# Key masks multiplied out on GpSimd, and the key scan split in two, in an attention and routing kernel

## What is computed

```python
feature_keep = min(HEAD_DIM, max(1, math.ceil(HEAD_DIM * (k_keep / Tx))))   # 16 * 64 / 1024 -> 1
q = _sparsify_last_dim_topk(proj(wq), feature_keep)   # one feature of 16 is kept
k = _sparsify_last_dim_topk(proj(wk), feature_keep)
v = _sparsify_last_dim_topk(proj(wv), feature_keep)
scores = einsum('bhqd,bhkd->bhqk', q, k) / sqrt(HEAD_DIM)       # causal
topk_vals, topk_idx = top_k(scores, 64)                         # 64 keys for each query
attn = softmax(scatter(topk_vals, topk_idx))
out = einsum('bhqk,bhkd->bhqd', attn, v)
```

## Time and profile before

| | before |
|---|---|
| median of 3 runs | 1072.18 us (1070.66 to 1073.46) |
| the profiled execution | 1072.58 us, of which the span from first to last instruction is 1070.7 us |
| attention part, 16 groups | some 66 to 730 us of the span |
| experts | from some 740 us to the end |
| granted TensorE clock, mean | 0.912 |

### The profile page before, as it was taken

How to read it: one execution, slowest core, us unless ns; L and a number is a source line. 1 busy time by engine, 2 the same in 40 slices (tenths; PEclk the granted TensorE clock), 3 DMA queues, 4 the chain that set the end, 5 groups by cost and what they waited for, 6 DMA issues and landing times. The chain is left out here.

```text
span 1070.7 us, 17237 instructions
## 1 busy us (share of the span) xinstructions
PE 919.0 (86%) x6504; PEld 497.5 (46%) x6504; DVE 662.1 (62%) x1462; ACT 480.0 (45%) x631; POOL 270.0 (25%) x403
## 2 busy tenths in 40 slices
PE   6778999898999888999999999996213999999996
PEld 4533443334444453534335445335102666666664
DVE  6758667567677666686784784625486655543441
ACT  2635667764667746476665554661000122221110
POOL 3503212411322402132320210001003433334222
PEclk9779999999999989999988998897555999999999
DMA  4000000000100001100002012001651144442211
GB/s 149 10 1 21 1 21 1 2 1 2 60 21 1 1 27 56 60 1 2 2 1 81 2 41 81 1 1 40 219 197 41 46 114 105 113 114 40 25 20 20
DMA packets 34854, 46.57 MB, mean 43 GB/s; under 512 B 2184, under 2 KB 30928, under 8 KB 34640
## 3 DMA queue, kind: packets, MB, share of 16 engines
q1 hardware_dynamic: 28624, 36.89, 10.3%
q0 software_dynamic: 6144, 8.52, 4.9%
HBM read 32.69 MB, written 12.72 MB: 42 GB/s over the span
## 5 line engine op out<-in xcount | busy, mean ns | idle before, releaser
L947 ACT ACTIVATE p_buf<-ps 128x1024 f32<-128x1024 f32 x288 | 279.4, 1023 | 182.7 <-PE ps L424 98.7
L424 PE MATMUL ps<-qx,kd 32*128 32x512 f32 (+3 forms) x1280 | 149.0, 542 | 29.9 <-DVE p_buf L1281 26.1
L457 PE MATMUL ps<-p_buf,vv 128*17 128x512 f32 (+3 forms) x1664 | 160.2, 487 | 0.0
L2096 ACT ACTIVATE h_t<-ps,b_t 128x512 f32<-128x512 f32 x64 | 44.0, 687 | 239.7 <-PE ps L2036 239.7
L1281 DVE SCALAR_TENSOR_TENSOR p_buf<-ps,p_buf 128x1024 f32<-128x1024 f32 x64 | 76.7, 1220 | 76.6 <-ACT p_buf L947 63.5
L2036 PE MATMUL ps<-tok_t,w_sb 128*128 128x512 f32 x256 | 114.2, 605 | 0.5 <-DVEq L2143 0.5
L2046 PE MATMUL ps<-w_sb,h_t 128*128 128x256 f32 x512 | 112.5, 380 | 0.8 <-ACT h_t L2096 0.8
L779 POOL TENSOR_SCALAR_AFFINE_SELECT p_buf<-p_buf 128x512 f32<-128x512 f32 x64 | 42.0, 669 | 274.2 <-ACT p_buf L947 271.5
L2046 PEld LDWEIGHTS ps<-w_sb,h_t 128*128 128x128 f32 x512 | 96.6, 190 | 15.3 <-ACT h_t L2096 1.6
L424 PEld LDWEIGHTS ps<-qx,kd 32*128 32x128 f32 x1280 | 55.8, 193 | 72.5 <-issue 57.1
L365 PE MATMUL ps<-w_t,h_t 128*128 128x512 f32 (+1 forms) x224 | 78.8, 496 | 0.8 <-ACT w_t L889 0.8
(11 more groups left out here) (293 smaller groups left out, 1392.9 us busy)
## 6 DMA issues: line engine op xcount, KB each, us to landing
w_sb<-in_L_ffn_w_dram SPq DMA_DIRECT2D x16, 1024.0 KB, 8.5
h_table<-xr SPq DMA_DIRECT2D x3, 1056.0 KB, 4.6
x_in<-in_L_attn_x_dram SPq DMA_DIRECT2D x6, 512.0 KB, 3.9
out_dram<-xr SPq DMA_DIRECT2D x3, 1024.0 KB, 5.2
xr<-in_L_attn_x_dram SPq DMA_DIRECT2D x3, 1024.0 KB, 5.7
h_table<-xr SPq DMA_DIRECT2D x2, 528.0 KB, 3.1
xr<-in_L_attn_x_dram SPq DMA_DIRECT2D x2, 512.0 KB, 5.4
p_buf<-in_L_wmod_dram SPq DMA_DIRECT2D x1, 1024.0 KB, 8.6
```

The lines of the kernel that those rows point to most:

```text
L424: m = pe.matmul(o, key, qx[r, par, t0:t0 + w], start=True, stop=not early)
L457: m = pe.matmul(ps[32 * h:32 * h + HD + 1, 6, o:o + w], vv[:, (gi // NG) % 2, i, HG * (gi % NG) + h, :], p_of(gi, u)[:, h, lo:lo + w], sta ...
L947: act.activation(p_of(gi, u)[:, 2 * a:2 * a + 2, :], buf(w), ACT.Exp, scale=0.25).then_inc(free_of(w)[0], 1)
L2096: act.activation(h1_t[:, f, :], ps[:, L1_BANKS[f % 3], :], ACT.Relu, bias=b1_t[:, e * FO + f:e * FO + f + 1]).then_inc(s_h1, 1)
```

## The change

The work stays what it was; its order on VectorE changes, and one piece goes to GpSimd.

- `key_counts` becomes `counts_first` (tokens 0 to 511, once K0 is there), in front of the masks `mask(gi, 1, 0)` and `mask(gi, 1, 1)`, and `counts_second` (512 to 1023, carried on), behind the masks and behind `one_feature(b + 1, t0 + 1)`, which went behind the masks too.
- `keys` becomes `key_maxima` and `keys_shifted`. `key_maxima` begins with two small [128, 128] masks, `k_yes` and `k_neg`, and signals `f_yes`. GpSimd's new `key_kinds(n)` waits for that and multiplies them out over the heads into `k_one` and `k_opp`. It stands behind `tri(gi, 2)` and `tri(gi, 3)`, in front of `stage` and of `keep(b + 1, t0 + 1)`. `keys_shifted` waits for it (`f_kinds`) before it shifts `ks` and `kx`.
- `out_rows_of(gi, 0)` stands between the two halves of `keys`; `normalize(b + 1, 0)` follows it. `zero_rank` comes before `queries`, and `losers` before `one_feature(b + 1, t0 + 3)` and `feature_limits`.

```diff
@@ -185,6 +185,8 @@
         l_max = sf("l_max", [P, NT])
 
         onesz = sf("onesz", [P, HG, P], BF16)
+        k_yes = sf("k_yes", [P, P], BF16)
+        k_neg = sf("k_neg", [P, P], BF16)
         sgn = sf("sgn", [P, 1])
         identb = sf("identb", [P, P], BF16)
         take = sf("take", [P, P], BF16)
@@ -223,6 +225,7 @@
         NU = len(UNITS)
         GA = B * NG
         FIRST = (1, 4)
+        f_yes, f_kinds = sem("f_yes"), sem("f_kinds")
 
 
         ring_at, m_at, pv_at = {}, {}, {}
@@ -780,6 +783,14 @@
                         lo += w
                     m.then_inc(f_tri, 1)
 
+                def key_kinds(n):
+                    pool.wait_ge(f_yes, n)
+
+                    pool.wait_ge(f_mfull, m_at["W", n - 1] + 1)
+                    pool.tensor_tensor(k_one[:, :, :], k_yes[:, :].unsqueeze(1).to_broadcast([P, HG, P]), onesz[:, :, :], ALU.mult)
+                    pool.tensor_tensor(k_opp[:, :, :], k_neg[:, :].unsqueeze(1).to_broadcast([P, HG, P]), onesz[:, :, :], ALU.mult)
+                    pool.drain().then_inc(f_kinds, 1)
+
                 def keep(b, t):
                     pool.wait_ge(f_one, NT * b + t + 1)
                     pool.wait_ge(*free_of(("Y", b, t)))
@@ -861,6 +872,8 @@
                         keep(b + 1, t0)
                     tri(gi, 2)
                     tri(gi, 3)
+                    if gi + 1 < GA:
+                        key_kinds(gi + 1)
                     if g == 0 or g == 3 and pre:
                         stage(gi + 2)
                     if tiles:
@@ -1216,31 +1229,45 @@
                     dve.tensor_tensor(y_most[:, :], y_most[:, :], y_ext[:, 2:3], ALU.max)
                     dve.drain()
 
-                def key_counts(n):
-                    kx = kd[:, n % 2, :]
+                def counts_first(n):
+                    h = slice(0, 512)
+                    dve.wait_ge(f_mfree, m_at["K0", n] + 1)
+                    dve.tensor_scalar(k_not[:, h], kd[:, n % 2, h], 0.0, None, ALU.is_le)
+                    dve.drain()
+                    dve.tensor_tensor_scan(left[:, h], k_not[:, h], minus1[:, :].to_broadcast([P, 512]), TOPK + 0.5,
+                                           ALU.add, ALU.add)
+
+                def counts_second(n):
+                    h = slice(512, T)
                     dve.wait_ge(f_mfree, m_at["K1", n] + 1)
-                    dve.tensor_scalar(k_not[:, :], kx, 0.0, None, ALU.is_le)
-                    dve.drain()
-                    dve.tensor_tensor_scan(left[:, :], k_not[:, :], minus1[:, :].to_broadcast([P, T]), TOPK + 0.5,
+                    dve.drain()
+                    dve.tensor_copy(carry[:, :], left[:, 511:512])
+                    dve.tensor_scalar(k_not[:, h], kd[:, n % 2, h], 0.0, None, ALU.is_le)
+                    dve.drain()
+                    dve.tensor_tensor_scan(left[:, h], k_not[:, h], minus1[:, :].to_broadcast([P, 512]), carry[:, :],
                                            ALU.add, ALU.add)
                     dve.drain().then_inc(f_cnr, 1)
 
-                def keys(n):
-                    par = n % 2
-                    kx = kd[:, par, :]
+                def key_maxima(n):
+                    kx = kd[:, n % 2, :]
+                    dve.tensor_scalar(k_yes[:, :], kx[:, 0:P], 0.0, None, ALU.is_gt)
+                    dve.tensor_scalar(k_neg[:, :], ks[:, n % 2, :], 0.0, None, ALU.is_lt).then_inc(f_yes, 1)
+
 
                     dve.tensor_tensor_scan(mx[:, :], kx[:, 0:512], kx[:, 0:512], 0.0, ALU.max, ALU.max)
                     dve.tensor_reduce(k_max1[:, :], kx[:, 512:T], AX.X, ALU.max)
                     dve.tensor_scalar(k_far[:, :], k_not[:, :], -FAR, None, ALU.mult)
                     dve.tensor_tensor(n_lo[:, :], n_lo[:, :], left[:, T - 1:T], ALU.min)
                     dve.scalar_tensor_tensor(kb[:, :], k_not[:, 0:P], FAR, kx[:, 0:P], ALU.mult, ALU.add)
-                    dve.scalar_tensor_tensor(k_one[:, :, :], kx[:, 0:P].unsqueeze(1).to_broadcast([P, HG, P]), 0.0,
-                                             onesz[:, :, :], ALU.is_gt, ALU.mult)
-                    dve.scalar_tensor_tensor(k_opp[:, :, :], ks[:, par, :].unsqueeze(1).to_broadcast([P, HG, P]), 0.0,
-                                             onesz[:, :, :], ALU.is_lt, ALU.mult)
                     dve.drain()
                     dve.tensor_tensor(k_max[:, :], mx[:, 511:512], k_max1[:, :], ALU.max)
-                    dve.drain()
+
+                def keys_shifted(n):
+                    par = n % 2
+                    kx = kd[:, par, :]
+                    dve.drain()
+
+                    dve.wait_ge(f_kinds, n)
                     dve.tensor_scalar(ks[:, par, :], ks[:, par, :], k_max[:, :], None, ALU.subtract)
                     dve.scalar_tensor_tensor(kx, kx, k_max[:, :], k_far[:, :], ALU.subtract, ALU.add).then_inc(f_kp, 1)
 
@@ -1447,42 +1474,46 @@
                     if gi:
                         out_rows_of(gi - 1, 1)
                     if more:
-                        key_counts(n)
-                    if g == 0 and pre:
-                        normalize(b + 1, 0)
+                        counts_first(n)
+                    mask(gi, 1, 0)
+                    mask(gi, 1, 1)
                     if tiles:
                         one_feature(b + 1, t0 + 1)
-                    mask(gi, 1, 0)
-                    mask(gi, 1, 1)
+                    if more:
+                        counts_second(n)
                     if post and g == norm_group(b - 1):
                         second_norm(b - 1, 1)
                     if g == 1 and pre:
                         norm_stats(b + 1, 1)
                     if more:
-                        keys(n)
-                    if tiles:
-                        one_feature(b + 1, t0 + 2)
+                        key_maxima(n)
                     out_rows_of(gi, 0)
+                    if g == 0 and pre:
+                        normalize(b + 1, 0)
                     if g == 0 and post:
                         take_mod(b - 1)
                     if gi == GA - 1:
                         take_mod(b)
                     if more:
-                        queries(n)
+                        keys_shifted(n)
+                    if tiles:
+                        one_feature(b + 1, t0 + 2)
                     if g == 0 and post:
                         residual(b - 1, 0)
                     if more:
                         zero_rank(n)
+                    if more:
+                        queries(n)
                     if g == 1 and pre:
                         normalize(b + 1, 1)
                     if g == 0 and pre:
                         modulate(b + 1, 0)
+                    if more:
+                        losers(n)
                     if tiles:
                         one_feature(b + 1, t0 + 3)
                     if g == 3 and pre:
                         feature_limits(b + 1)
-                    if more:
-                        losers(n)
                     if g == 0 and post:
                         residual(b - 1, 1)
                     if g == 1 and pre:
```

## The result

| | before | changed |
|---|---|---|
| median | 1071.42 us (1070.46 to 1073.46, 4 runs) | 1108.65 us (1107.96 to 1113.41, 4 runs) |
| ratio, 95% interval | | 1.0356 [1.0330, 1.0382] |
| span of the profiled execution | 1070.7 us | 1106.9 us |
| granted TensorE clock, mean | 0.912 | 0.910 |

The kernel became 37.2 us slower; 1114 was forecast, in a range of 1090 to 1130. The page of the changed kernel, part 1, answers the earlier trace rows: busy us, share of the span, instructions.

A forecast was written before the change was run, and what follows sets the result against it. PE, busy 86%, has to be fed; it waits mostly for VectorE's masks, and ACT's eviction chain has no slack. 37.8 + 3.0 + 9.1 - 8.6 = 41.3 us on 1072.6 gave about 1114 us, range 1090 to 1130.

The forecast's parts named there:

- Part 1: PE's score matmuls waiting for masks: masks come sooner, some 20 of 26.1 us to be had if nothing else ends late.
- Part 2: VectorE's own work: k_one and k_opp leave, k_yes and k_neg cost 0.2 each; about 0.8 us less a group.
- Part 3: GpSimd's products beside key_maxima hold VectorE off: some 1.7 us lost, key_maxima about 4.6 us, not 2.9.
- rival (c): As forecast, but GpSimd's multiplications take 2 us each or one-element operations wait too: 1122 to 1130 us; chance 0.17.
- Rival (a): VectorE and GpSimd don't hold each other off in key_maxima, or GpSimd gets in before the scan: 1097 us; chance 0.20.
- Part 4: Six tile groups: key_kinds delays GpSimd's keep, so ACT's eviction and PE's S7 come late; 37.8 us longer in all.
- Part 5: PE's clock: after pauses PE works for a few us at its lower level in tile groups; 3.0 us more.
- Part 6: Groups without tiles: VectorE's longer path adds 9.1 us in gi=0, 3, 7, 11, 13; gi=4, 8, 12, 14 win 8.6.
- The signs: Six ACT waits for keep of 4 to 8 us; masks' wait about 6 us; losers' wait over 10 us.
- Rival (b): Faster: key_kinds is through before ACT reaches tile t0+2's eviction, needing f_yes before about 295.6; 1053 us; chance 0.09.

The follow-up runs named there:

- number 6: The changed kernel with k_yes, k_neg and their signal moved from key_maxima to the end of counts_first, ahead of the masks; 1066.61 us, ratio 0.9950.
- Number 1: The changed kernel with GpSimd's key_kinds moved behind keep(b + 1, t0 + 1); 1088.45 us, ratio 1.0172.
- number 3: Against number 2: both waits kept, key_kinds in front of keep, but holding only a one-column product that nobody reads; 1102.41 us, ratio 1.0300.
- Number 4: The kernel before, in its old order, with GpSimd's part alone added (key_kinds in front of keep); 1082.64 us, ratio 1.0125.
- number 2: The changed kernel's new order on VectorE alone: VectorE makes k_one and k_opp, GpSimd has no part; 1078.87 us, ratio 1.0081.
- number 5: Number 1, but VectorE makes its own k_one and k_opp, and GpSimd's two products go into unread tensors; 1116.18 us, ratio 1.0400.

## Why the prediction was right

- **Part 1, the masks.** "Some 20 of the 26.1 us": 19.1 (26.1 to 7.0), in gi=5 from 0.72 to 0.37. Right.
- **Part 2, VectorE's own work.** Smaller than charged for a handover that is placed well: in gi=5 of number 6 `k_yes` and `k_neg` cost nothing, since VectorE waits 3.1 us behind them. At 0.22 each in `key_maxima` the 0.2 were right.
- **Part 3, side by side.** The forecast took `key_maxima` at 4.6 us where 2.9 would do. The trace has 0.27 from `k_yes` to the scan and behind it 4.25 us in most groups without tiles and 4.86 in tile groups, 4.5 and 5.1 together. The forecast was right in size, in part for another reason: it left out that the one-element operations wait. They do, `n_lo` for 1.0 us in all 15 groups and `k_max` for 1.0 where `keep` follows, while `k_far`, which the forecast had wait for GpSimd, lost only 0.3. The Trainium skill's page "SBUF — State Buffer", section "Who interferes with whom", says this of VectorE instructions with two SBUF inputs; the trace agrees, 1104 ns against 149. The 8 us that rival (c) had for this did not come on top: they took the place of the wait of `k_far`, on which the forecast had put most of its 1.7. The other half of (c), products of 2 us, is false: alone they take 1.16, as the row of `keep` said. `key_kinds` was through 3.6 us after `f_yes` where 4.1 was forecast. Rival (a), no hold-off, falls with the 2.00 us of `k_one` in all 15 groups.
- **Part 4, the wait in front of `keep`.** The mechanism, the place and the six times are as forecast. On the clock of gi=5, whose masks now start at 309.21 where 292.38 was, S7 was forecast 7.5 us late; it waits 7.18, where before it did not wait. In g = 1 it is +20.4 against +19.8. In g = 2 it is +17.5 against 21.0: S7 waits 4.93 us in each of the three where 5.4 was forecast, and "almost nothing is absorbed" was too much (together the groups came out 3.5 us shorter than forecast), and the 1.2 us for `pv(gi, 8)` behind `one_feature(t0+3)` measured 1.0 (3.1 in 3). Number 1 confirms the place: 20 us. What the prediction did not see is that `keep` and `stage`, once late, run beside `key_maxima` (numbers 1 and 3). Number 4 adds what the prediction did not separate: that GpSimd's part costs 12 us in the old order and 29 in the new one.
- **Part 5, the clock.** 3.0 us was forecast, for the two tile groups that still ran at a granted clock of 1.00. PE's busy time in the six tile groups rises by 4.1 (246.3 to 250.4 over the windows of the cut): 1.6 in gi=5 and 1.5 in gi=6, which are the 3.0, and 1.0 in the other four, which the sum had at nothing.
- **Part 6, groups without tiles.** The four between are +8.8 for +6.9, gi=4, 8 and 12 -6.4 for -7.8. The first of these is near for some luck: gi=0 is +4.1 for +2.0 and gi=3 +2.4 for +1.3, but gi=11 +0.5 for +1.8. Mis-sized is gi=13, +2.2 forecast and -0.5 measured: PE's busy time in its window fell from 38.81 us at a granted clock of 0.88 to 37.23 at 0.92, a gain of 1.6 us which the sum did not have; why the clock was better there was not followed. What lies outside the groups with keys to make (start, 14, 15 and the experts) was put at -0.8 and was -3.5: the start is 1.2 us longer, and what lies behind gi=13 is 4.8 shorter (404.5 to 399.7), with 6.7 us less of PE's busy time for the same matmuls (321.1 to 314.4, at a granted clock of 0.87 and 0.88). These last two are 5.4 of the 5.1 us by which the forecast was too high; the rest cancels, which is luck.
- **The signs.** Six waits of ACT for `keep` are there, at 6.4 to 8.6 us, and the wait for the masks is 7.0 for the 6 forecast. The wait for `losers` (line 1267 before, 1294 now) did not grow to over 10 us; it is 8.8. What grew was the one for `out_rows_of`, from 3.2 to 12.6, whose path part 6 had priced but which the signs did not name.
- **Rival (b)**, faster because `key_kinds` is through before ACT needs the buffer, named its own condition: `f_yes` before about 295.6 on the clock of gi=5 before, about 3 us behind the masks' start. Number 6 puts the signal 3 us in front of them and is faster, at 1066.6; the price of 1053 that went with it was too hopeful by some 14: PE still waits 11.4 us for `out_rows_of`, which stands behind `counts_second`, and 11.7 for `losers`, where it waited 3.2 and 4.8 before.

What stays open: how number 3's 23.5 us divide between the late `keep` and the longer `key_maxima`, and what makes the work behind gi=13 shorter or longer. The new order as such does not explain that: it takes 404.5 us in the kernel before, 398.3 in number 2 and 398.0 in number 6, but 406.2 in number 5, which has the same order on VectorE.

## What to carry to other kernels

An in-order queue makes each wait a wait for everything behind it: before handing work to an idle engine, ask when its signal comes and what is queued behind it, and give the signal where its inputs are first ready, not where its result is first wanted. Ask also what the delayed work will then run beside: here it held VectorE off. An engine that is busy only a quarter of the time may still stand between two others with no slack. And judge a move in every kind of group: `out_rows_of` in front of `key_maxima` cost 0.5 us in gi=5 and 4.4 in gi=4, and the kernel 28 in all.

## What the runs showed of the hardware

- VectorE operations on one element of each partition, with two inputs from SBUF, waited for a whole GpSimd product: 1104 ns on average for `n_lo`, against 149. The Trainium skill's page named above states it; its size, a sevenfold price for the smallest instructions of the list, had not been expected.
- An operation with one input waits as well. In number 6, the comparison `k_not` (line 1247), 0.42 us alone, took 1.35 beside GpSimd's `keep`:

```profile
295.90 1.16 POOL L800 TENSOR_TENSOR qk<-y_val,y_one 128x512 f32<-128x512 f32 x1 [5.16 <-DVE y_one L1217]
...
295.99 1.35 DVE L1247 TENSOR_SCALAR k_not<-kd 128x512 bf16<-128x512 f32 x1
```

- PE's busy time for the same matmuls is no constant: it was 901.8 us in number 6, at a mean granted clock of 0.930, and 930.6 in number 5, at 0.903. Of the 53.0 us between these two spans 28.8 are that.
